# Mamba block and mixture of experts in one kernel: token rows stored in three parts and joined in the routed stage, 1/sqrt on ScalarE, another softplus form and another order of items

## The reference

```python
h = _layernorm(x) * (1 + ca) + sa
# selective scan over 512 channels with 16 states each
xs, res = split(h @ in_proj_w.T)             # 512 + 512
xs = silu(conv4(xs) + conv_b)
dt, B, C = split(xs @ x_proj_w.T)            # 64, 16, 16
delta = softplus(dt @ dt_proj_w.T + dt_proj_b)
state = exp(delta * A) * state + (delta * xs) * B    # per token
y = (state . C) * silu(res)
x = x + ga * (y @ out_proj_w.T)
h = _layernorm(x) * (1 + cb) + sb
gates = [top 1 of 7 routed experts, 1 shared expert]
x = x + gb * sum over e of gates[e] * ((silu(h @ W1b[e]) * (h @ W1a[e])) @ W2[e])
```

## Time and profile before

| | us |
|---|---|
| median of 3 runs | 2519.82 |
| lowest and highest | 2518.24, 2520.49 |
| time of the profiled execution | 2518.41 |
| its span in the trace | 2516.4 |
| TensorE, VectorE, ScalarE, GpSimd busy | 2129.4, 1929.2, 1390.9, 1956.2 |
| fused program, first to last scan | from about 70 to 1943 |
| routing program and its loads | from about 2012 to 2066 |
| routed tiles | from about 2071 to the end |

### The profile page before, as it was taken

How to read it: one execution, slowest core, us unless ns; L and a number is a source line. 1 busy time by engine, 2 the same in 40 slices (tenths; PEclk the granted TensorE clock), 3 DMA queues, 4 the chain that set the end, 5 groups by cost and what they waited for, 6 DMA issues and landing times. The chain is left out here.

```text
span 2516.4 us, 34344 instructions
## 1 busy us (share of the span) xinstructions
PE 2129.4 (85%) x9216; PEld 1004.0 (40%) x9217; DVE 1929.2 (77%) x2060; ACT 1390.9 (55%) x2488; POOL 1956.2 (78%) x840
## 2 busy tenths in 40 slices
PE   7668988888888898888888888888866649999997
PEld 3223333333334343433333433334232335656654
DVE  2699999999999999999999999999998162222222
ACT  3566666667585857666666667585745232222221
POOL 1899898999989889999899898989898014555553
PEclk9778879888889888988989798988888869999999
DMA  5443342424242424334242424342331062222221
...
DMA packets 149416, 224.66 MB, mean 89 GB/s; under 512 B 48227, under 2 KB 85617, under 8 KB 145138
## 3 DMA queue, kind: packets, MB, share of 16 engines
...
...
## 5 line engine op out<-in xcount | busy, mean ns | idle before, releaser
L1052 POOL TENSOR_TENSOR hs<-hs,c_rep 128x2048 f32<-128x2048 f32 x256 | 1154.5, 4530 | 81.8 <-ACT state L795 81.8
L892 DVE TENSOR_TENSOR_SCAN hs<-dA,state,hs 128x512 f32<-128x512 f32 x768 | 930.7, 1263 | 47.8 <-ACT dA L775 43.5
L775 ACT ACTIVATE dA<-d_rep,a 128x512 f32<-128x512 f32 x1024 | 687.9, 685 | 367.3 <-DVE hs L892 363.5
L1045 POOL TENSOR_TENSOR hs<-u_rep,b_rep 128x2048 f32<-128x2048 f32 x96 | 435.5, 4536 | 37.9 <-PE bank L537 37.9
L879 DVE TENSOR_TENSOR hs<-u_ps,b_rep 128x2048 f32<-128x2048 f32 x160 | 360.9, 2272 | 15.6 <-PE u_ps L527 10.5
L489 PE MATMUL bank<-n,w1s 128*128 128x512 f32 x512 | 273.7, 667 | 73.3 <-DVE delta L860 38.5
L892 DVE TENSOR_TENSOR_SCAN hs<-dA,hs 128x512 f32<-128x512 f32 x256 | 293.9, 1202 | 28.9 <-ACT dA L775 28.0
L537 PE MATMUL bank<-hs,spread 128*32 128x512 f32 x2048 | 276.1, 687 | 25.8 <-POOL hs L1052 22.4
L1437 DVE TENSOR_TENSOR hid<-z,sg 128x512 f32<-128x512 f32 x70 | 48.4, 692 | 297.8 <-ACT sg L1415 297.8
L1355 PE MATMUL z<-w1r,hT 128*128 x560 | 260.6, 608 | 2.9 <-issue 2.4
L448 PE MATMUL bank<-xin,w_in 128*128 128x512 f32 x512 | 245.3, 619 | 10.0 <-ACT xin L620 9.2
...
## 6 DMA issues: line engine op xcount, KB each, us to landing
d_rep<-delta SPq DMA_DIRECT2D x1024, 64.0 KB, 2.0
u_rep<-us SPq DMA_DIRECT2D x384, 64.0 KB, 2.0
...
xres<-in_x SPq DMA_DIRECT2D x16, 512.0 KB, 3.9
...
token_rows<-xres SPq DMA_DIRECT2D x16, 512.0 KB, 3.1
xin<-in_x SPq DMA_DIRECT2D x15, 512.0 KB, 9.5
```

Of the source, the lines that this page charges most:

```text
L775: nc.scalar.activation(dA[:, u % ABANK, :], d_rep[:, q, :], ACT.Exp, scale=t["a"][:, u:u + 1]).then_inc(da_ready, 1)
L892: nc.vector.tensor_tensor_scan(hs[:, s % RING, g, :], dA[:, u % ABANK, :], hs[:, s % RING, g, :], state[:, u:u + 1] if m else 0.0, ALU.mul ...
L1045: nc.gpsimd.tensor_tensor(hs[:, s % RING], u_rep[:, i % UBUF, :].unsqueeze(1).to_broadcast([P, NG, T]), b_rep[:, par, :].rearrange("p (g t ...
L1052: nc.gpsimd.tensor_tensor(hs[:, s % RING, :, :], hs[:, s % RING, :, :], c_rep[:, par, :].rearrange("p (g t) -> p g t", g=NG), ALU.mult).th ...
```

## The change

It has five parts.

1. The fused program stores a token's row as three parts of 256: the normalized row without scale and shift (`store_n2`), the residual (`store_x1`) and the gated output of the shared expert without gb (`store_acc`). `RB`, `scale` for w2, `W2` and `load_w2s` go. `Y` is evicted by ScalarE with the gate as its scale; `accumulate` goes. `T2` waits until n2 is stored, since it overwrites it.
2. In the routed tiles GpSimd gathers rows of 3 x 256 and modulation rows of 3 x 256 (sb, 1 + cb, gb). VectorE makes the modulated row before `turn` (`modulate`) and joins the three parts in `combine`.
3. 1/sqrt(v + eps) is exp(-0.5 ln(v + eps)) on ScalarE (`V`, `V2`); the shift is made by VectorE (`SH`, `SH2`).
4. softplus(z) is max(min(ln(1 + exp(z)), 40), z): `DT` takes exp(z) at once and `exp_delta` goes.
5. All tables have a new order.

```diff
         plan = {
-            5: [(('OP', 0), -1), (('CV', 2), 1), (('CV', 3), 1), (('OP', 1), -1), (('RS', 0), 1), (('RS', 1), 1), (('SUM', 0), 0), (('XP', 0), 1)],
+            5: [(('CV', 2), 1), (('OP', 1), -1), (('CV', 3), 1), (('RS', 0), 1)],
...
         evict = {
-            4: [[], [], [], [(('CV', 1), 1), (('CV', 2), 1)]],
+            4: [[(('CV', 0), 1)], [], [(('CV', 1), 1)], []],
+            5: [[], [(('CV', 2), 1), (('CV', 3), 1)], [], [(('HALO', 0), 2)]],
...
-        transfers = [('W2', 0), ('ACC2', 0), ('U', 5), ('D', 4), ('XR', 0), ('D', 6), ('U', 7), ('D', 5), ('D', 8), ('U', 10), ('WO', 0), ('D', 7),
+        transfers = [('U', 5), ('ACC2', 0), ('D', 6), ('XR', 0), ('D', 4), ('D', 5), ('U', 7), ('D', 7), ('WO', 0), ('U', 10), ('D', 8), ('ROWS', 0), ('D', 10), ('D', 9), ('D', 13),
+                     ('U', 13), ('D', 11), ('U', 15), ('D', 14), ('D', 12), ('X', 0), ('LOG', 0), ('D1', 0), ('X1', 0), ('D', 15), ('U1', 2), ('BC', 0), ('D1', 1), ('D1', 3), ('D1', 2)]
...
-            def store_rows(f):
-                hold(sp, back_kept, 2 * f + 2, held)
-                for i in range(2):
-                    sp.dma_start(rows_out[0, f][:, 2 * i:2 * i + 2, :], hid[:, 2 + i, :].rearrange("p (h d) -> p h d", h=2)).then_inc(rows_stored, 16)
+            def store_n2(f):
+                hold(sp, n2_ready, f + 1, held)
+                sp.dma_start(rows_out[0, f], n2[:]).then_inc(n2_stored, 16)
+
+            def store_x1(f):
+                hold(sp, x1_ready, 2 * f + 2, held)
+                sp.dma_start(rows_out[1, f], xres[:]).then_inc(x1_stored, 16)
...
-                    nc.scalar.activation(delta[:, j, :], ps_[:, :], ACT.Abs).then_inc(abs_ready, 1)
+                    nc.scalar.activation(delta[:, j, :], ps_[:, :], ACT.Exp).then_inc(exp_ready, 1)
...
+                elif kind == "Y":
+                    if j == 0:
+                        act.wait_ge(gate_ready, f + 1)
+                        act.wait_ge(x1_stored, 16 * (f + 1))
+                    for h in range(2):
+                        tt = 2 * j + h
+                        last = nc.scalar.activation(xres[:, tt, :], ps_[:, h * D:(h + 1) * D], ACT.Copy, scale=gs[:, 1, tt:tt + 1])
+                    last.then_inc(acc_ready, 1)
...
+            def deviation2(f):
+                act.wait_ge(stats2_ready, f + 1)
+                nc.scalar.activation(rstd2[:], mv2[:, :, 1], ACT.Ln, bias=t["eps"][:, 0:1]).then_inc(rstd2_step, 1)
+                act.wait_ge(rstd2_step, f + 1)
+                nc.scalar.activation(rstd2[:], rstd2[:], ACT.Exp, scale=-0.5).then_inc(rstd2_ready, 1)
...
+            def offset(f):
+                dve.wait_ge(rstd_ready, f + 1)
+                nc.vector.scalar_tensor_tensor(out=shift[:], in0=mv[:, :, 0], scalar=-1.0, in1=rstd[:], op0=ALU.mult, op1=ALU.mult).then_inc(shift_ready, 1)
...
-                nc.vector.scalar_tensor_tensor(out=delta[:, j, :], in0=ps_[:, :], scalar=0.0, in1=delta[:, j, :],
-                                               op0=ALU.max, op1=ALU.add).then_inc(delta_ready, 1)
+                nc.vector.scalar_tensor_tensor(out=delta[:, j, :], in0=delta[:, j, :], scalar=LINEAR, in1=ps_[:, :],
+                                               op0=ALU.min, op1=ALU.max).then_inc(delta_ready, 1)
...
             def turn(k, q, n):
-                pe.wait_ge(fetched[q], 32 * n + 32)
+                pe.wait_ge(mod_ready, k + 1)
...
-                nc.vector.scalar_tensor_tensor(out=outr[:, q, :], in0=y_ps[:, :], scalar=cur[:, q, 3:4].bitcast(F32), in1=gbr[:, q, :],
-                                               op0=ALU.mult, op1=ALU.mult).then_inc(y_used, 1)
+                nc.vector.scalar_tensor_tensor(out=outr[:, q, :], in0=y_ps[:, :], scalar=cur[:, q, 3:4].bitcast(F32), in1=rows[:, q, 2 * D:3 * D],
+                                               op0=ALU.mult, op1=ALU.add).then_inc(y_used, 1)
                 dve.wait_ge(y_used, k + 1)
+                nc.vector.tensor_tensor(outr[:, q, :], outr[:, q, :], mods[:, q, 2 * D:3 * D], ALU.mult).then_inc(weighed, 1)
+                dve.wait_ge(weighed, k + 1)
                 nc.vector.tensor_tensor(outr[:, q, :], outr[:, q, :], rows[:, q, D:2 * D], ALU.add).then_inc(out_ready, 1)
+
+            def modulate(k, q, n):
+                dve.wait_ge(fetched[q], 32 * n + 32)
+                nc.vector.tensor_tensor(rows[:, q, 0:D], rows[:, q, 0:D], mods[:, q, D:2 * D], ALU.mult).then_inc(mod_step, 1)
+                dve.wait_ge(mod_step, k + 1)
+                nc.vector.tensor_tensor(rows[:, q, 0:D], rows[:, q, 0:D], mods[:, q, 0:D], ALU.add).then_inc(mod_ready, 1)
...
                 nc.vector.tensor_tensor(hid[:, q % 2, :], z[:, q % 2, 0, :], sg[:, q % 2, :], ALU.mult).then_inc(hid_ready, 1)
+                if not is_last(k, 2):
+                    modulate(*at(2))
                 if not first(k, 1):
                     combine(*at(-1))
```

More of the change, by code:

```diff
@@ L361, in transfer @@
                     load_w_out(c // CPB)
-                elif kind == "W2" and m == 1 and not (known(c) and c == 1):
-                    hold(sp, out2_made, 2 * (c - 1), held)
-                    load_w2s(c // CPB)
                 elif kind == "ROWS":
-                    store_rows(c - 1)
+                    store_n2(c - 1)
+                elif kind == "X1":
+                    store_x1(c - 1)
                 elif kind == "LOG":
@@ L820, in _ @@
             save(NCHUNK - 1, NSET - 1)
-            for item in [item for s in range(NSET) for part in evict[s] for item in part]:
-                if item[1] == -1 or item[0][0] == "SRS":
-                    do(item, NCHUNK, 0)
+            for c in (NCHUNK, NCHUNK + 1):
+                for item in [item for s in range(NSET) for part in evict[s] for item in part]:
+                    if item[1] < 0 or (item[0][0] == "SRS" and c == NCHUNK):
+                        do(item, c, c % CPB)
         @block.vector
@@ L947, in do @@
                     hidden(f, j)
-                elif kind == "Y":
-                    accumulate(f, j)
                 elif kind == "RC":
@@ L955, in do @@
                     layernorm2(f)
+                elif kind == "SH":
+                    offset(f)
+                elif kind == "SH2":
+                    offset2(f)
             def body(c, m):
@@ L967, in _ @@
             layernorm(0)
+            offset(0)
             dve.wait_ge(selectors, 1 + NF)
@@ L993, in _ @@
             nc.vector.tensor_scalar(t["cb2"][:], cols2_ps[:, KD:2 * KD, :], 1.0, None, ALU.add).then_inc(cols_kept, 1)
+            offset(1)
             for h in range(2):
```

234 lines of the change are left out of this document (100 added, 134 removed), and 40 rows, old and new, of tables (evict, plan).

## The result

The changed kernel takes 2619.7 us (median of four runs, 2613.2 to 2627.9) against 2519.2 (2518.2 to 2520.5): 1.040 times as long, 95% interval 1.037 to 1.043. The forecast was 2555, the range 2503 to 2610. The sign was right; the size, +100 for +35, was not, and the time lies above the range. The profiled execution of after took 2613.15 us, the fastest of the four; its span is 2611.1.

The account below looks back on a forecast made before the run. VectorE was taken to bound the scan stage, TensorE the routed tiles. 2518.4 - 19.2 (scan stage) - 1.4 + 53.7 (routed tiles) + 2.0 = 2553.5; with 1.4 for the median, 2555 us, range 2503 to 2610.

Parts of the forecast that it names:

- I cost these at nothing: Scan stage, SP's queue: the stores and loads moved in its list were taken as covered, costing nothing.
- 1/sqrt leaves GpSimd: Scan stage: 1/sqrt moves to ScalarE, which has room; GpSimd isn't the bound, so costed at nothing.
- Waits that the order moves: Scan stage: 3.6 us of VectorE's waits a chunk go, 1.6 come; net -2.0, bounds -3.6 and 0.
- Work: Scan stage, VectorE: accumulate's 1.9 us a chunk goes, SH and SH2 bring 0.3; -1.4 us taken.
- Port: Scan stage: the small operations wait for GpSimd at the shared SBUF port; net +2.2 us a chunk, bounds 0 and 9.1.
- Routed tiles: Transposes wait for the modulation behind hid, closing a ring of 6.87 us instead of 6.08; 68 x 0.79 = +53.7 us.
- First and last tile: Routed tiles: two operations and larger fetches before the first transposes +1.5, longer last combine +0.5; together +2.0 us.
- Behind the last scan: 2.2 us of GpSimd's chain become 0.8 us on ScalarE and VectorE; -1.4 us.
- C: Rival, 0.18: issuing a gather holds the port in routed tiles too, another 0.56 us a tile; 2593 us.
- B: Rival, 0.16: scan stage's waits go and the small operations don't wait, 4.4 us a chunk gained; 2504 us.
- D: Rival, 0.05: the modulation in the routed tiles is hidden, so the 53.7 us don't come; 2501 us.
- E: Rival, 0.04: TensorE falls to half clock in the routed tiles' gaps, z 5.66 instead of 3.69 us; 2691 us.

Follow-up runs that it names:

- l: Kernel before with the load of the next chunk's input moved later in SP's list, behind D 12 instead of BC; 2585.1 us.
- c: Changed kernel with each small operation written as four of 128x1, 1/sigma as per-partition scalar instead of a second SBUF tensor; 2612.8 us.
- a: Changed kernel with the load of the next chunk's input five items earlier in SP's list, behind D 13; 2586.8 us.
- d: Changed kernel with the edits of a, b and c together; 2846.4 us, its routed tiles slowed as in b.
- h: Kernel of a with ScalarE's 1/sigma of the next chunk ahead of the two silus instead of behind them; 2579.9 us.
- i: Kernel of h with the edits of g and c added; 2522.2 us, 1.001 times the kernel before.
- j: Kernel of i with TensorE's read of the expert's number ahead of the row transposes; 2509.1 us, 0.996 times the kernel before.
- n: Kernel of j with GpSimd's two fetches of a tile exchanged, modulation rows first; 2495.5 us, 0.990 times the kernel before.
- g: Changed kernel with the modulation of the tile two ahead issued ahead of hid instead of behind it; 2561.6 us.
- b: Changed kernel with the modulation issued one tile further ahead, still behind hid; 2896.4 us.
- e: Changed kernel with TensorE's read of the expert's number for z ahead of the row transposes; 2581.8 us.

## Why the prediction was right in sign and wrong in size

By the spans the forecast missed 59.6 us (94.7 for 35.1): 43.3 in the scan stage, 4.7 behind it and 11.6 in the routed tiles. The scan stage, us a chunk (in "inside the small operations" 0.14 us of each are taken off as its work; the forecast's chunk counts 0.8 of its 3.0 as covered):

| | before | l | after | c | a | d | h | forecast |
|---|---|---|---|---|---|---|---|---|
| chunk | 117.6 | 122.3 | 119.1 | 119.3 | 117.5 | 116.6 | 116.9 | 116.3 |
| VectorE stands | 7.1 | 11.6 | 8.2 | 9.3 | 7.7 | 6.8 | 7.1 | 4.9 |
| of it for xin | 0 | 4.1 | 4.0 | 4.0 | 0 | 0 | 0 | 0 |
| inside the small operations | | | 1.9 | 0 | 0.7 | 0 | 0.7 | 3.0 |

- **"I cost these at nothing" on SP's queue: the step that failed.** The text walked along the list for `D`, `T2`, `X1` and `BC`, and left out the load X. It stood ahead of `ROWS` and stands now behind it and eight more items. Walked like the others: the store is issued and the queue free at 1192.95, eight items of four issues take 2.7 us each (21.6), one of them waits 5.1 us for ScalarE, and the landing takes 4.0: 1223.7, for statistics that wanted to begin at 1223.82 - 4.87 = 1218.95. Without the 5.1 us the load would have landed just in time, so the walk has to take in the waits of the items ahead, too. In after this wait is 4.0 us a chunk for nothing in the forecast, while everything else that VectorE waits for fell by 2.9. Its price is another matter: a puts 22 us of the scan stage on it in this order by the traces, 33 us by the medians; l puts 66 us on it in the old order.
- **"1/sqrt leaves GpSimd", nothing: also missed.** ScalarE has room on average, but its 1/sigma stands behind two silus and a change of its table, and VectorE reads it right away. In after the late load hid this; in a it is a wait of 23.6/13 = 1.8 us a chunk. h removes it and gains 14 us by the traces and 7 by the medians, and d is as early without removing it. So the wait is shown, its price is not.
- **Waits that the order moves, -2.0 a chunk:** each named wait went as written, 3.6 us, and the new ones in after are `DB` and `OP` with the 1.6 given. But h, without the late load, stands 7.1 us a chunk as before: once the load no longer held VectorE, waits for exponentials and sums came back, and the term is 0.
- **Work, -1.4: right.** In h VectorE is busy 109.8 us a chunk for 110.5 before, with 0.7 us of waiting inside its small operations; without that -1.4.
- **Port, +2.2 (0 to 9.1):** mechanism shown, by the ends that agree within 0.03 us wherever a small operation was long, by the 4.43 us in a, and by c, which is free of it. The rule of the Trainium skill ("SBUF — State Buffer", section "SBUF: two separate sides"), that of the two the one that starts first holds the shared ports for its whole instruction, holds here. The size was 1.9 us of waiting for the 3.0 taken in after and 0.7 in a and h: how long it is hangs on where GpSimd's product stands just then, and does not come at random as the text took it. Its net price was nothing where `A 0` waited for TensorE in its place (c for after), 0.9 us a chunk in the order of a (d for a, one trace each), and nothing in that of h (116.9 in h, 116.8 to 117.1 in i, j and n). So the price is small and not settled; the forecast was too high.
- **The sum for h is partly luck.** Its -0.7 us a chunk is near the -1.2 forecast, but by two misses that cancel: waits 0 for -2.0, port +0.7 for +2.2.
- **Routed tiles, +53.7: right mechanism, 7.5 us too small.** The closed ring was as written, and g opens it; 68 x 0.90 is 61.2. The modulation ended 0.79 us behind hid (2306.39 - 2305.60), not 0.92, which leaves the transposes 0.64 us late. What the term lacked was the read of the expert's number: 0.20 us of "issue" and 0.06 of the transposes behind the wait. With the read out of the way on both sides the tiles are 6.51 and 5.82 us: the ring costs 0.69.
- **First and last tile, +2.0: too small.** From the routing's last operation to the first z it is 13.2 instead of 11.1 us: +2.1, inside the 0.9 to 3 of the text. But behind the first z another 65.8 - 68 x 0.90 = 4.6 us belong to no tile of the steady ring, where the text had 0.5; 3.8 of them are the first two tiles, which ran at granted clocks of 0.68 and 0.87 for 0.75 and 1.00 before.
- **Behind the last scan, -1.4:** +4.8 instead of +0.1 up to the first z in this trace. In the nine traces of a, b, c, d, e, g, h, i and j the same stretch is 128.1 to 129.7 us, where after has 132.8 and before 128.0. So the forecast of +0.1 holds for them within 2 us. About 3 us more stand only in after and in n (131.5), ahead of the store of the last rows, and were not taken apart.
- **Rivals.** C fell: the modulation ran 0.41 us at 2305.52 while the gather's issue went from 2305.00 to 2305.95, and of the 70 first operations of the modulations 64 overlap such an issue, none longer than 0.43 us. B's first half happened and wasn't enough. D needs the modulation ahead of hid (g). E fell, the clock was 1.00 in the steady tiles; its price was too small in any case, since the z of 5.66 us that it was read from ran at 0.65, not at half. A's own bounds for the fused stage, -3.4 to +2.5 us a chunk, don't follow from its terms, which give -5.0 to +7.7; the measured +1.5 lies inside both.

So the +24 of the scan stage is one wait of 4.0 us a chunk that the text had at nothing, against 2.9 of others that fell. That the load's place makes this wait is shown both ways, by a and l. Not settled is what keeps the stage from the -19 of the forecast once the load is early: by their traces a has +2, h -12 and d -14, but i, j and n, with both edits, -5 to -9, and the medians of a and h differ by 7 only.
